# The keys' scaling by minus beta issued on GpSimd instead of VectorE

## What is computed

```python
q = l2norm(silu(h @ Wq)); k = l2norm(silu(h @ Wk)); v = silu(h @ Wv)
beta = sigmoid(h @ Wb) * 2.0
def step(S, ...):                       # one time step, per head, 16 wide
    pred = S^T k_i
    S = S + beta_i * k_i (v_i - pred)^T
    o = S^T q_i
```

## Time and profile before

| | |
|---|---|
| median of 3 runs (lowest, highest) | 839.27 us (836.18, 839.94) |
| the profiled execution's own time | 836.87 us |
| its span, first to last instruction | 835.1 us |
| mean granted TensorE clock | 0.833 of full |
| busy: TensorE matmul | 651.5 us, 78% |
| busy: VectorE | 479.5 us, 57% |
| busy: ScalarE | 247.5 us, 30% |
| busy: GpSimd | 94.6 us, 11%, 127 instructions |
| chain that ended last, by engine | TensorE 63%, VectorE 23%, ScalarE 3%, GpSimd 2% |

### The profile page before, as it was taken

How to read it: one execution, slowest core, us unless ns; L and a number is a source line. 1 busy time by engine, 2 the same in 40 slices (tenths; PEclk the granted TensorE clock), 3 DMA queues, 4 the chain that set the end, 5 groups by cost and what they waited for, 6 DMA issues and landing times.

```text
span 835.1 us, 15890 instructions
## 1 busy us (share of the span) xinstructions
PE 651.5 (78%) x6704; PEld 439.9 (53%) x6704; DVE 479.5 (57%) x1164; ACT 247.5 (30%) x543; POOL 94.6 (11%) x127
## 2 busy tenths in 40 slices
PE   3348375317858999969599699979688889999995
PEld 2125233314757887746569587678344334444442
DVE  4472864446787845465782863374666764444443
ACT  1113022027524143255354204313333122222221
POOL 1323235123000001111110001010111000000000
PEclk9578677758565999999876856995899999999998
DMA  9990000220000000000000005000000000000001
GB/s 351 306 388 19 25 0 0 49 28 0 2 2 2 3 4 2 2 2 2 1 2 2 2 2 162 2 1 2 1 1 1 0 0 1 13 8 6 0 1 26
DMA packets 13314, 29.59 MB, mean 35 GB/s; under 512 B 2272, under 2 KB 7008, under 8 KB 12992
## 3 DMA queue, kind: packets, MB, share of 16 engines
q1 hardware_dynamic: 13248, 28.64, 10.7%
HBM read 26.54 MB, written 2.10 MB: 34 GB/s over the span
## 4 chain that ended last, share of the span: by engine, by line
PE 63%; DVE 23%; DMA 3%; ACT 3%; issue 2%; POOL 2%; SPq 2%; DVEq 0%; POOLq 0%; ACTq 0%
PE psum L712 6%; PE psum L721 6%; PE psum L707 6%; PE psum L644 5%; PE psum L553 4%; PE psum L519 3%; PE psum L670 3%; PE psum L673 3%; PE psum L633 2%; DMA zlast<-in_ctx_last 2%; PE psum L580 2%; PE psum L424 2%; PE psum L499 2%; PE psum L626 2%; POOL rstd L899 2%
## 5 line engine op out<-in xcount | busy, mean ns | idle before, releaser
L879 ACT ACTIVATE arena<-psum 128x512 f32<-128x512 f32 x68 | 40.5, 597 | 139.4 <-PE psum L707 124.3
L1316 DVE TENSOR_TENSOR arena<-psum,arena 128x512 f32<-128x512 f32 x64 | 44.2, 691 | 57.9 <-PE psum L712 54.7
L721 PE MATMUL psum<-arena,wed_sb 128*128 128x512 f32 x128 | 67.2, 606 | 0.0
L424 PE MATMUL psum<-ident,yn 128*128 128x128 f32 x88 | 19.4, 375 | 60.9 <-DVE yn L975 30.8
L1320 DVE TENSOR_TENSOR arena<-psum,arena 128x512 f32<-128x512 f32 x64 | 44.3, 691 | 27.6 <-PE psum L721 27.4
L739 ACT ACTIVATE arena<-psum 128x512 f32<-128x512 f32 x56 | 33.3, 599 | 68.9 <-PE psum L519 40.4
L424 PEld LDWEIGHTS psum<-ident,yn 128*128 128x128 f32 x88 | 14.0, 191 | 65.5 <-DVE yn L975 33.8
L899 POOL TENSOR_TENSOR rstd<-ve,neg_half 128x4 f32<-128x4 f32 x44 | 46.7, 1062 | 3.5
L519 PE MATMUL psum<-arena 32*64 32x128 f32 x1024 | 41.6, 325 | 7.0 <-ACT arena L739 3.5
L898 POOL TENSOR_TENSOR ve<-ss,eps_rms 128x4 f32<-128x4 f32 x20 | 4.5, 223 | 345.2 <-ACT yr L772 252.6
L519 PEld LDWEIGHTS psum<-arena 32*64 32x64 f32 x1024 | 36.5, 164 | 12.9 <-ACT arena L739 4.7
(11 more groups left out here) (252 smaller groups left out, 1337.9 us busy)
## 6 DMA issues: line engine op xcount, KB each, us to landing
arena<-in_ctx_t SPq DMA_DIRECT2D x16, 514.0 KB, 8.6
arena<-in_ctx_z SPq DMA_DIRECT2D x16, 512.0 KB, 9.5
XA<-in_x SPq DMA_DIRECT2D x1, 1024.0 KB, 4.9
zlast<-in_ctx_last SPq DMA_DIRECT2D x4, 256.0 KB, 16.2
x_mid<-XA SPq DMA_DIRECT2D x2, 512.0 KB, 2.6
X<-x_mid SPq DMA_DIRECT2D x8, 128.0 KB, 4.8
weg_sb<-in_we_gate SPq DMA_DIRECT2D x2, 512.0 KB, 6.8
weu_sb<-in_we_up SPq DMA_DIRECT2D x2, 512.0 KB, 7.6
```

What stands on the lines that cost most here:

```text
L424: last = pe.transpose(bank[:, jj * D:(jj + 1) * D], src[u][:, jj, :], ident[:, :])
L721: pe.matmul(x3, wed_sb[:, (p - 1) % (NPAIR + 1), :], act_a[pr], start=(p == 0), stop=False, skip_group_check=True).then_inc(x_down[pr], 1)
L879: act.activation(act_g[pr], banks[4 * pr], ACT.Silu).then_inc(x_silu[pr], 1)
L1316: dve.tensor_tensor(act_gu[pr], banks[4 * pr + 1], act_g[pr], ALU.mult).then_inc(x_gu[pr], 1)
```

## The change

The scaling by minus beta leaves VectorE's part of the step `kq`, with the wait ahead of it, and becomes GpSimd's part of the same step, behind a wait for `q_k`. It reads and writes the same tiles in the same shapes. TensorE's "a" steps get a wait for `q_kb`. `STEPS` stays as it is.

```diff
--- before.py
+++ after.py
@@ -608,6 +608,7 @@
                         half = int(kind[2])
                         pe.wait_ge(l_out[u], pi + 1)
                         pe.wait_ge(q_vb, i + 1)
+                        pe.wait_ge(q_kb, i + 1)
                         blocks((b0, b1)[half], half, TT[g], KV[g]).then_inc(s_a[u], 1)
                     elif kind == "wt":
                         pe.wait_ge(s_ae[u], pi * 2 + 2)
@@ -947,6 +948,11 @@
                                            qkv[g][:, :, 2 * D:3 * D].rearrange("p j (h e) -> p j h e", h=H),
                                            bc(beta[g][:, :, :].unsqueeze(3), [P, GT, H, DK]),
                                            ALU.mult).then_inc(q_vb, 1)
+                    elif kind == "kq":
+                        pool.wait_ge(q_k, i + 1)
+                        pool.tensor_tensor(kv_part(g, 0).rearrange("p j (h e) -> p j h e", h=H),
+                                           KH[g].rearrange("p (j h e) -> p j h e", j=GT, e=DK),
+                                           bc(nbeta[g][:, :, :].unsqueeze(3), [P, GT, H, DK]), ALU.mult).then_inc(q_kb, 1)
                     elif kind == "n2":
                         pool.wait_ge(m_ss, i + 1)
                         rsqrt(st, g, ss[g][:, 0:GT], GT, eps_rms, m_rr)
@@ -1217,10 +1223,6 @@
                                           ALU.mult)
                         dve.tensor_tensor(KH[g].rearrange("p (j h e) -> p j h e", j=GT, e=DK), qk[:, :, H:2 * H, :],
                                           bc(rn[:, :, H:2 * H].unsqueeze(3), [P, GT, H, DK]), ALU.mult).then_inc(q_k, 1)
-                        dve.wait_ge(q_k, i + 1)
-                        dve.tensor_tensor(kv_part(g, 0).rearrange("p j (h e) -> p j h e", h=H),
-                                          KH[g].rearrange("p (j h e) -> p j h e", j=GT, e=DK),
-                                          bc(nbeta[g][:, :, :].unsqueeze(3), [P, GT, H, DK]), ALU.mult).then_inc(q_kb, 1)
                     elif kind[:4] == "gram":
                         q = int(kind[4])
                         dve.wait_ge(g_a[u], pi * 4 + q + 1)
```

## The result

The changed kernel takes 843.91 us (median of 20 runs, 840.59 to 847.25), the kernel before 839.42 us beside it: a ratio of 1.0049, 95% interval 1.0031 to 1.0068. It is slower by 2.6 to 5.7 us. The forecast was 841.3, slower by 2.0. The profiled execution has a span of 843.2 us. It starts 3.7 us late already at 205 us, ahead of every changed instruction, so its span alone says nothing of the change; stretches between two landmarks do. The page first: busy times as in the earlier trace rows, with 9 us more on GpSimd and little less on VectorE, because what is held up counts as busy.

The account below looks back on a forecast made before the run. TensorE, busy 78% of the span, was taken to lead the chain (63%), VectorE next (23%). Terms +0.31 - 0.67 + 2.35 + 0 = +2.0 us over the median 839.27 gave 841.3 us; range 836.0 to 846.5.

Parts of the forecast that it names:

- the four parts: The `kq` steps of layers 1 and 2, streams A and B: +0.31, -0.67, +2.35 and 0 us.
- layer 2 B: `kq` of layer 2, stream B: TensorE busy without a break from 434 to 447 us covers any saving or loss.
- Layer 1 A: `kq` of layer 1, stream A: small L1208 and L1209 held by GpSimd's second scaling, sum of squares L1211 later, +0.31 us.
- Layer 1 B: `kq` of layer 1, stream B: `ext` starts earlier, -0.67 us; +0.23 should L1227 be held too.
- L1218 held by GpSimd: In `kq`, GpSimd's first scaling holds VectorE's second-group L1218, which ends 0.43 us after it; 1.4 us instead of 0.68.
- rival 1: VectorE is never held by GpSimd, GpSimd alone waits: sum +0.8, 840.1 us; chance 0.16.
- Layer 2 A, the queue: `kq` of layer 2, stream A: GpSimd's scalings stand ahead of `rsqrt` for `n2` of B, delaying TensorE's `mtr`, +2.35 us.
- The sum of the terms: All `kq` steps and the wait for `q_kb`: +0.31 - 0.67 + 2.35 + 0 = +2.0 us.
- The clock: TensorE's stretch behind the delayed `mtr` in layer 2, stream A: expected at full clock, 1.00.
- rival 2: TensorE's clock falls behind the delayed `mtr`: 1.7 us more, 843.0, or 847.4 with 256 small matmuls; chance 0.22.
- rival 3: The shift brings L553 of layer 2, stream B, to full clock: 835.2 us; chance 0.09.

Follow-up runs that it names:

- changed_again: The changed kernel, unaltered, measured once more with a second trace; ratio to the kernel before 1.0054.
- only_2a: Against the changed kernel, only the `kq` step of layer 2, stream A, scales on GpSimd, the other three on VectorE; ratio to the kernel before 1.0068.
- all_but_2a: Against the changed kernel, layer 2, stream A, scales on VectorE again, the other three `kq` steps on GpSimd; ratio to the kernel before 0.9979.
- behind_n2: The changed kernel, but in layer 2, stream A, GpSimd issues its scalings in step `kt0`, behind `n2` of stream B; ratio to the kernel before 1.0003.
- filled: The changed kernel with six filler matmuls on TensorE ahead of its wait in `mtr` of stream B; ratio to the kernel before 1.0025.
- both_keys: The changed kernel, but GpSimd waits in all four `kq` steps for both groups' keys before its first scaling; ratio to the kernel before 1.0073.

## Why the prediction was right or wrong

- The places: right. The four `kq` steps behave as the four parts said; layer 2 B costs nothing.
- Layer 1 A: +0.31 forecast, +0.10 measured (5.46 to 5.56). Right was that a small instruction of `sq` is held; which one, and by what, was not. The forecast had L1208 and L1209 of the first group held by the second scaling. They got in ahead of it, and the first sum of squares came earlier, against the forecast's own sign: 3.71 us after `kq` instead of 4.04, and 3.46 in `changed_again`. Held was L1214 of the second group, 0.59 us, by GpSimd's beta times v. The forecast saw that this comes later and called it needed only by ScalarE much later; that it would hold VectorE was overlooked. That the term came out small is in part luck.
- Layer 1 B: -0.67 forecast, -0.59 measured (5.06 to 4.47). L1227 was not held.
- L1218 held by GpSimd: right, against rival 1. It takes 1.55 us, not 1.42: it ends 0.55 us after GpSimd does, where 0.43 was worked out from the 128-wide L975. The Trainium skill's rule in "Who interferes with whom" (SBUF — State Buffer), that a VectorE instruction with two SBUF inputs contends with a GpSimd instruction that reads SBUF, agrees with the trace, 0.68 to 1.55 us.
- Layer 2 A, the queue: +2.35 forecast, +2.52 measured (5.58 to 8.10), and in four traces the same. `only_2a`, `all_but_2a` and `behind_n2` show it by itself.
- The sum of the terms: +2.0 forecast, 0.10 - 0.59 + 2.52 = +2.03 in the traces.
- The clock: here the forecast chose wrongly. Its sign was a clock of 1.00 in the stretch behind `mtr`, and it was 0.50. I gave 0.45 to the sum alone and 0.22 to rival 2, the fall behind the stall; in all traces with the stall and no filler, five of five, the clock fell. It was also sized too small: 1.7 us for one stretch of 3.4 us, where the half clock lasted 6.8 us and cost 3.3. `filled` shows that it comes from TensorE standing: with work in the same gap it does not fall.
- From 2.03 + 3.3 = 5.3 us to the 4.5 us between the medians: partly given back. In the trace, L553 of layer 2 B took 12.6 us instead of 13.75; its first 64 matmuls took 2.06 us, the pace of the full clock. In `changed_again` it took 13.3, so 1.1 us came back in one execution and 0.5 in the other. That such places give and take is rival 3's mechanism.
- 841.3 against 843.91, within the range, though the main forecast had left out the larger of the two costs; 0.67 stood for "the same" and 0.24 for slower by over 0.5%, and the measured +0.49% lies at that border. Rival 2's own time, 843.0 with one stretch, is the nearest of all.

## What to carry to other kernels

An engine with 12% load can still be on the path at one moment: before giving it work in a fixed order, look at who waits for what stands behind that work, at each of its places; here one place of four lost 2.5 us and the clock's 3.3 behind it, and the same edit, issued two steps later in the list there, lost 0.4 us and no clock. Look also at what the queue pushes back: beta times v, 1 us later, held an instruction that nobody had moved. A stall on TensorE should be priced twice, as time and as the clock of what follows, and the second price was the larger here. Moving work from VectorE to GpSimd gave little where the two then ran side by side: in layer 1, +0.10 and -0.59 us where VectorE's own relief would have been -0.61 and -1.17.

## What the runs showed of the hardware

- The engines do not meet only at semaphores: VectorE and GpSimd alternate by whole instructions where both read SBUF. GpSimd's scaling, started while VectorE's L1222 runs, waits for its end (1.44 instead of 1.06 us), then goes ahead of VectorE's next, L1224, which had started on paper and takes 1.55. A small VectorE instruction of 32 columns, L1214, was held for 0.42 us by GpSimd's beta times v and ended 0.03 us after it; `ext`'s L1236 with two SBUF inputs took 1.72 instead of 1.16 us in `both_keys`. L1229, with one input in PSUM, kept 0.68 us beside GpSimd.
- TensorE's clock can be worth more than what moves it: the same 256 matmuls of step `o` took 7.7 us at full clock and 13.0 at half, and a change of 0.43 us over 100 us earlier went with a gain of 9 us over the kernel before. A cause between the two is not shown.
- The distances of the table repeat to 0.06 us between traces wherever the code around them is the same (4.47 us eight times, 8.10 four times), while the first `kq` starts anywhere from 203.9 to 211.1 us. Small changes are better read from the former.
